# Node attention of a decoder: angle remainders moved from VectorE to GpSimd, mask matmuls of two query tiles in two row groups

## What is computed

```python
logits = (x @ wr).reshape(B, N, H, K_NODES).transpose(0, 2, 1, 3)
tk_vals, tk_idx = jax.lax.top_k(logits, TOP_K)
tk_w = jax.nn.softmax(tk_vals, axis=-1)
member = jax.nn.one_hot(tk_idx, K_NODES, dtype=jnp.float32).sum(axis=-2) > 0
pos = jnp.cumsum(m_i, axis=2) - m_i          # place of a token in its node
for n in range(K_NODES):
    p = pos[..., n]
    c = cos_c[p]
    s = sin_c[p]
    qr = q * c + _rotate_half(q) * s
    kr = k * c + _rotate_half(k) * s
    ...
```

## Time and profile before

| | us |
|---|---|
| median of 3 runs | 1866.5 (1866.48 to 1873.33) |
| the profiled execution, its own time | 1868.13 |
| its span, first to last instruction | 1866.4 |
| TensorE busy over the span | 1387.0 (74%) |
| VectorE busy | 1109.8 (59%) |
| ScalarE busy | 709.0 (38%) |
| GpSimd busy | 443.9 (24%) |
| mean granted TensorE clock | 0.863 of full |

### The profile page before, as it was taken

The page is one execution under the profiler, slowest core; times in us unless marked ns, Lnnn a source line. Parts: engine busy times, 40 slices in busy tenths (PEclk is TensorE's granted clock), DMA queues, the critical chain, the costliest instruction groups (busy, mean ns, idle before and its releaser), DMA issues. The chain is left out here.

```text
span 1866.4 us, 25316 instructions
## 1 busy us (share of the span) xinstructions
PE 1387.0 (74%) x9045; PEld 1055.8 (57%) x9045; DVE 1109.8 (59%) x2340; ACT 709.0 (38%) x1529; POOL 443.9 (24%) x464
## 2 busy tenths in 40 slices
PE   4898898888866897774765956758616878869785
PEld 3676666666745564561444955546513756646663
DVE  5899999999446577224566545352454827425534
ACT  4456666656222464221321221013203333634351
POOL 2565566565210100120101310000001015002300
PEclk8899899998878799786887977669868989989897
DMA  6111111010010100430002500000200002000100
GB/s 217 28 35 36 27 41 35 27 41 15 1 58 1 35 1 1 141 116 0 1 13 101 181 17 1 1 1 1 88 3 1 1 1 43 2 0 18 27 2 12
DMA packets 31612, 64.01 MB, mean 34 GB/s; under 512 B 6784, under 2 KB 18176, under 8 KB 30976
## 3 DMA queue, kind: packets, MB, share of 16 engines
q1 hardware_dynamic: 30464, 60.15, 10.4%
q0 software_dynamic: 1024, 2.23, 0.5%
HBM read 54.13 MB, written 4.18 MB: 31 GB/s over the span
## 5 line engine op out<-in xcount | busy, mean ns | idle before, releaser
L188 POOL TENSOR_TENSOR rstd<-spread,minus_half 128x4 f32<-128x4 f32 x36 | 36.9, 1024 | 913.2 <-DVE spread L170 913.2
L918 PE MATMUL l0h_scores<-l0h_k_rot,l0h_q_slots 128*128 128x128 f32 (+1 forms) x1024 | 208.2, 351 | 0.0
L918 PEld LDWEIGHTS l0h_scores<-l0h_k_rot,l0h_q_slots 128*128 128x128 f32 x1024 | 171.2, 210 | 13.3
L1135 POOL TENSOR_TENSOR l0h_k_part<-large_weights,l0h_sines 128x512 f32<-128x512 f32 x64 | 84.0, 1313 | 177.8 <-PE l0h_scores L918 129.8
L1009 ACT ACTIVATE l0h_scores<-l0h_scores,l0h_top 128x128 f32<-128x128 f32 (+1 forms) x256 | 100.6, 393 | 26.3 <-DVE l0h_top L1088 26.2
L1082 DVE TENSOR_TENSOR l0h_q_slots<-l0h_q_rot,l0h_chosen 128x1024 f32<-128x1024 f32 x64 | 78.4, 1225 | 6.7
L894 PE MATMUL l0h_projected<-XT,l0h_wq 128*128 128x256 f32 x256 | 70.1, 397 | 15.8 <-ACT large_weights L980 11.8
L1136 POOL TENSOR_TENSOR l0h_k_rot<-large_weights,l0h_cosines 128x512 f32<-128x512 f32 x64 | 81.0, 1266 | 0.0
L908 PE MATMUL l0h_scores<-l0h_key_masks,l0h_query_picks 4*128 4x128 bf16 (+1 forms) x256 | 45.2, 258 | 47.7 <-DVE l0h_probs L1105 47.7
L1447 ACT ACTIVATE l0n_probs<-l0n_scores,l0n_top 128x256 f32<-128x256 f32 x128 | 53.9, 483 | 38.9 <-DVE l0n_top L1478 38.7
L1088 DVE TENSOR_REDUCE l0h_top<-l0h_scores 128x2 f32<-128x256 f32 (+1 forms) x128 | 65.0, 546 | 5.4 <-PE l0h_scores L918 5.4
(11 more groups left out here) (761 smaller groups left out, 3703.6 us busy)
## 6 DMA issues: line engine op xcount, KB each, us to landing
l1e_experts<-in_l_experts SPq DMA_DIRECT2D x16, 768.0 KB, 4.3
l0e_experts<-in_l_experts SPq DMA_DIRECT2D x15, 578.0 KB, 3.9
l0h_chosen<-l0h_chosen_dram SPq DMA_DIRECT2D x64, 128.0 KB, 3.0
small_weights<-in_w_l_ffn SPq DMA_DIRECT2D x1, 4016.0 KB, 12.2
l0h_pos<-l0h_pos_dram SPq DMA_DIRECT2D x56, 64.0 KB, 2.1
large_weights<-in_w_l_xattn SPq DMA_DIRECT2D x1, 2632.0 KB, 9.1
l3f_late<-l3f_values SPq DMA_DIRECT2D x2, 1040.0 KB, 7.0
l0h_wq<-in_l_wq SPq DMA_DIRECT2D x16, 128.0 KB, 3.0
```

The lines of the kernel that those rows point to most:

```text
L918: mm = nc.tensor.matmul(at[:, slot], q_slots[:, s % 2, slot, part, i * P:(i + 1) * P], k_rot[:, s % 2, part, 0:KEYS[i][1]], start=False, s ...
L1135: nc.gpsimd.tensor_tensor(k_part[:], source, at_batch(sines, s), ALU.mult)
```

## The change

1. The remainders (`reduce_turns`) go from VectorE to GpSimd. VectorE keeps them for heads 0 and 1, before the loop. For heads 2 to 15 GpSimd computes them behind `rotate_k(s)` at b = 0 of the head before; until now VectorE did it at the end of the head two before.
2. On ScalarE `fold(h + 1)` stands at b = 0 (before: `fold(h + 2)` at b = 3), and `sines_of(h + 1)` at b = 1 (before: b = 0).
3. The masks lie twice in SBUF, at partitions 0 to 3 and 64 to 67. `load_masks` makes four transfers instead of two. The four mask matmuls of a step stand together ahead of both tiles, in the order tile 0, tile 1, tile 0, tile 1; tile 0 reads rows 0 to 3, tile 1 rows 64 to 67.

```diff
--- before.py
+++ after.py
@@ -787,8 +787,9 @@
         pos = sb("pos", [P, N], BF16)
         spread = sb("spread", [ROWS0, 2, NODES, FREQS], BF16)
         chosen = sb("chosen", [P, 2, CHOICES, N], BF16)
-        key_masks = sb("key_masks", [NODES, 2, N], BF16)
-        query_picks = sb("query_picks", [NODES, 2, CHOICES, N], BF16)
+        key_masks = sb("key_masks", [P // 2 + NODES, 2, N], BF16)
+        query_picks = sb("query_picks", [P // 2 + NODES, 2, CHOICES, N], BF16)
+        rows_of_tile = lambda i: slice(i * P // 2, i * P // 2 + NODES)
         cosines, sines = sb("cosines", [P, 2, N]), sb("sines", [P, 2, N])
         k_both = k.large_tail[:, 0:2 * N].rearrange("p (a n) -> p a n", a=2)
         k_rot, k_part = sb("k_rot", [P, 2, 2, S]), sb("k_part", [P, 2, S])
@@ -842,11 +843,12 @@
                 def load_masks(h):
                     if h >= 2:
                         sp.wait_ge(scores_ready, 2 * (h - 1) * B)
-                    sp.dma_start(key_masks[:, h % 2], absent_dram[h * NODES:(h + 1) * NODES])\
-                        .then_inc(masks_loaded[h % 2], 16)
-                    sp.dma_start(query_picks[:, h % 2],
-                                 chosen_dram[:, h * NODES:(h + 1) * NODES].rearrange("o r s -> r o s"))\
-                        .then_inc(masks_loaded[h % 2], 16)
+                    for i in range(TB):
+                        sp.dma_start(key_masks[rows_of_tile(i), h % 2], absent_dram[h * NODES:(h + 1) * NODES])\
+                            .then_inc(masks_loaded[h % 2], 16)
+                        sp.dma_start(query_picks[rows_of_tile(i), h % 2],
+                                     chosen_dram[:, h * NODES:(h + 1) * NODES].rearrange("o r s -> r o s"))\
+                            .then_inc(masks_loaded[h % 2], 16)
 
                 sp.dma_start(chosen_dram.rearrange("o r s -> r o s"), chosen_t[0:ROWS0]).then_inc(routes_stored, 16)
                 sp.dma_start(absent_dram, absent_t[0:ROWS0, :]).then_inc(routes_stored, 16)
@@ -900,14 +902,16 @@
                     h, b = step(s)
                     if s >= 2:
                         pe.wait_ge(combined, s - 1)
-                    pe.wait_ge(masks_loaded[h % 2], 32 * (h // 2 + 1))
+                    pe.wait_ge(masks_loaded[h % 2], 64 * (h // 2 + 1))
+                    for slot in range(CHOICES):
+                        for i in range(TB):
+                            query = slice((TB * b + i) * P, (TB * b + i + 1) * P)
+                            rows = rows_of_tile(i)
+                            nc.tensor.matmul(unit(scores, s, i)[:, slot], query_picks[rows, h % 2, slot, query],
+                                             key_masks[rows, h % 2, b * S:b * S + KEYS[i][1]], start=(slot == 0),
+                                             stop=False, skip_group_check=True)
                     for i in range(TB):
                         at = unit(scores, s, i)
-                        query = slice((TB * b + i) * P, (TB * b + i + 1) * P)
-                        for slot in range(CHOICES):
-                            nc.tensor.matmul(at[:, slot], query_picks[:, h % 2, slot, query],
-                                             key_masks[:, h % 2, b * S:b * S + KEYS[i][1]], start=(slot == 0), stop=False,
-                                             skip_group_check=True)
                         nc.tensor.matmul(at[:, :, i * P:(i + 1) * P], k.above[:], bc(k.masker[:].unsqueeze(1), [P, 2, P]),
                                          start=False, stop=False, skip_group_check=True)
                         if i == 0:
@@ -1044,11 +1048,11 @@
                     if k_chunk_at(s) is not None:
                         copy_k(4 * (s // (G0 * B) + 1) + k_chunk_at(s))
                     if b == 0 and 1 <= h < H0 - 1:
+                        fold(h + 1)
+                    if b == 1 and 1 <= h < H0 - 1:
                         sines_of(h + 1)
                     if b == 2 and h + 2 < H0:
                         turns(h + 2)
-                    if b == 3 and h + 2 < H0:
-                        fold(h + 2)
                 copy_turned(STEPS - 1)
                 copy_out(STEPS - 2)
                 copy_out(STEPS - 1)
@@ -1116,8 +1120,6 @@
                     if s + 2 < STEPS:
                         rotate_q(s + 2)
                     combine(s)
-                    if b == 3 and h + 2 < H0:
-                        reduce_turns(h + 2)
 
             @block.gpsimd
             def _(g):
@@ -1137,13 +1139,22 @@
                     nc.gpsimd.tensor_tensor(k_rot[:, s % 2, 0], k_rot[:, s % 2, 0], k_part[:, 1], ALU.subtract)
                     nc.gpsimd.tensor_tensor(k_rot[:, s % 2, 1], k_rot[:, s % 2, 1], k_part[:, 0], ALU.add).then_inc(k_rotated, 1)
 
+                def reduce_turns(h):
+                    g.wait_ge(turns_ready, h + 1)
+                    link(g, nc.gpsimd.tensor_scalar(sines[:, h % 2], cosines[:, h % 2], ROUND, ROUND, ALU.add, ALU.subtract))
+                    nc.gpsimd.tensor_tensor(sines[:, h % 2], sines[:, h % 2], cosines[:, h % 2], ALU.subtract)\
+                        .then_inc(turns_reduced, 1)
+
                 k.gchain(g, nc.gpsimd.memset(spread[:], 0.0))
                 for h in range(2):
                     nc.gpsimd.affine_select(out=spread[:, h], in_=spread[:, h], compare_op=ALU.not_equal, fill=1.0,
                                             base=-NODES * h, pattern=[[-1, NODES], [0, FREQS]], channel_multiplier=1)\
                         .then_inc(spread_set, 1)
                 for s in range(STEPS):
+                    h, b = step(s)
                     rotate_k(s)
+                    if b == 0 and 1 <= h < H0 - 1:
+                        reduce_turns(h + 1)
```

## The result

The changed kernel takes 1895.5 us, median of 4 runs (1891.82 to 1896.45), against 1869.9 for the kernel before, 4 runs too. The ratio is 1.013, 95% interval 1.0094 to 1.0165. The forecast was 1829, with a range of 1820 to 1847. The profiled execution took 1891.8 us, its span is 1890.1, 23.7 longer than before. The sixty steps of the attention that took 418.9 us now take 444.5, 25.6 more, so all of the loss lies there.

What follows compares the result with a forecast made beforehand. VectorE's list of work was taken as the bound. Terms -34.0 (remainder), -10 (stalls), +4.5 (K heads) and +2 (sines), the others 0, sum to -37.5 us, so 1829 us, range 1820 to 1847.

Steps and rivals of the forecast that it cites:

- The bound: VectorE's own list of work sets the stage's length nearly everywhere, 6.17 us per undisturbed step.
- The remainder leaves VectorE: On VectorE, 14 remainders of 2.43 us each disappear from its queue: -34.0 us.
- Stalls behind the falling clock: TensorE idles during VectorE's remainder, its clock falls, VectorE then waits; removing this gives -10 us, bounds 0 and -12.
- K heads: Three heads where TensorE has the longer chain, project_q awaiting ScalarE's key copy; +4.5 us over three, bounds +2 and +9.
- rival B: Only the remainder's time returns: clock still falls, or ScalarE ties late with VectorE; 1844 us, chance 0.30.
- Sines one step later: On ScalarE, cosines end just before VectorE's next product wants them, 0.03 us slack; +2 us, bounds 0 and +8.
- D: Time origin of the prediction's sums: the start of VectorE's first product in step b = 1.
- GpSimd, 0 us up to R = 6.5: GpSimd's remainder delays the keys of b = 1 only beyond R near 6.5; 0 us, bounds 0 and +41.
- R: Time of GpSimd's rounding and difference together per remainder: 3.9 us, bounds 3.2 and 9.4.
- 2.4 us of lead: How far TensorE's scores end before VectorE is free for them, counted as slack for late keys.
- Masks, 0 outside the K heads: Four mask matmuls together save TensorE 0.2 to 0.3 us a step, inside its slack of 0.67: 0 us.
- C: GpSimd becomes the bound: slower from R = 9.8, chance 0.04; another 0.04 for ending near no change.

Runs made afterwards that it cites:

- best_old_masks: late_sines_first with the masks as in the kernel before (one copy, tile by tile); 1837.1 us, 0.981 of before.
- masks_only: The kernel before with the masks' part of the change alone, remainders still on VectorE; 1863.6 us, 0.995 of before.
- no_remainder: The changed kernel without the remainders of heads 2 to 15 on any engine, sines still at b = 1; 1848.9 us, 0.987 of before.
- late_sines_first: The changed kernel with GpSimd's remainder behind the keys of b = 1 and the sines ahead of ScalarE's two copies; 1831.6 us, 0.979 of before.
- late_remainder: The changed kernel with GpSimd's remainder behind the keys of b = 1 instead of b = 0; 1852.0 us, 0.991 of before.
- sines_first: The changed kernel with the sines at b = 1 moved ahead of ScalarE's two copies; 1890.1 us, 1.009 of before.

## Why the prediction was wrong

**The bound.** Right: VectorE's list of 6.17 us a step is the floor, and all kernels return to it wherever nothing is late.

**The remainder leaves VectorE, -34.0.** Right: ahead of b = 0 the excess goes from 33.7 to 0.7.

**Stalls behind the falling clock, -10.** Right in size and, where nothing else is late, in cause: best_old_masks has no remainder on VectorE, the old masks and a clock of 1.00, and its 3.4 us ahead of b = 2 all lie in the K heads. The masks alone take 9.5 us away as well, with the clock still falling (b = 2 in masks_only), so the two gains do not add up. In the changed kernel new idle time of TensorE took the place of the old. Against rival B the prediction held that the step with `turns` leaves TensorE no idle time of 2.9 us. Behind VectorE's wait for the cosines that step (from 308.02) left it just that, and the eight scores behind it take 3.58 us and not 1.89:

```profile
313.42 0.39 PE L910 MATMUL l0h_scores<-l0h_key_masks,l0h_query_picks 4*128 4x128 bf16 x4 [2.92 <-DVE l0h_probs L1109]
...
314.87 3.58 PE L922 MATMUL l0h_scores<-l0h_k_rot,l0h_q_slots 128*128 128x256 f32 x8
```

**Sines one step later, +2, measured 32.5 ahead of b = 2.** First failed step: "ScalarE does its exponents and copies, loads the table at D + 2.75". That was read in the one step where the remainder on VectorE had put TensorE ahead, and the change removes that remainder. In a step without that lead it is D + 4.1 with the new masks, which alone costs 25 us (no_remainder; 22 of them without the K heads' own 3). The other 7 or 8 us come from TensorE being later still behind GpSimd: in the changed kernel the table of the step of 299.72 is loaded at 304.53, 4.8 us in.

**GpSimd, 0 us up to R = 6.5, measured 40.9 ahead of b = 1 at R = 6.0.** Second failed step, in three parts. R itself was mis-sized: 6.0 for 3.9, since the rounding took 3.63 us where I took 1.5; inside the bounds 3.2 to 9.4. The start was wrong: D + 10.1 was the end of keys that begin with the sines at D + 6.14; they began at 308.05, D + 8.3, and the remainder also waits for `turns`, which the sum left out. So TensorE gets the keys of b = 1 at 322.75, D + 23.0, where the prediction's own sum with R = 6.0 gives D + 20.1. These rows of the changed kernel show both, and what came of it:

```profile
304.53 1.28 ACT L1004 ACT_TABLE_LOAD   x1
...
308.05 1.27 POOL L1137 TENSOR_TENSOR l0h_k_part<-large_weights,l0h_sines 128x512 f32<-128x512 f32 x1 [6.13 <-ACT l0h_cosines L1005]
...
311.45 1.16 ACT L995 ACTIVATE l0h_cosines<-l0h_pos,large_weights 128x1024 f32<-128x1024 bf16 x1
...
312.70 3.63 POOL L1144 TENSOR_SCALAR l0h_sines<-l0h_cosines 128x1024 f32<-128x1024 f32 x1 [0.68 <-ACT l0h_cosines L995]
...
318.73 1.26 POOL L1137 TENSOR_TENSOR l0h_k_part<-large_weights,l0h_sines 128x512 f32<-128x512 f32 x1
...
322.75 1.16 PE L922 MATMUL l0h_scores<-l0h_k_rot,l0h_q_slots 128*128 128x128 f32 x8 [1.92 <-POOL l0h_k_rot L1140]
...
326.56 1.03 PE L896 MATMUL l0h_projected<-XT,l0h_wq 128*128 128x256 f32 x4
```

And the slack was measured to the wrong consumer. I gave TensorE 2.4 us of lead, from the end of its scores to `find_top`. But `project_q` stands last in TensorE's iteration, and VectorE takes it up right after: before, it ended at 331.4 and the next product but for the remainder stood at 326.70 + 6.17 = 332.9, a lead of 1.5. Here it ends at 327.59, and the product waits until 327.63.

**Masks, 0 outside the K heads.** Right where nobody is late (best_old_masks), and 0.3 us a step in the K heads as reckoned. Wrong for the two kernels compared here: 10.8 us of steps in masks_only (418.9 to 408.1), and 13 us beside the moved remainders (457.5 to 444.5), where TensorE is the late one. Slack is worth nothing only while nothing draws on it.

**K heads, +4.5.** About right: +5.1. In late_sines_first they stand nearly alone: 8.3 us beyond the floor, 7.8 of it theirs, 2.5 to 2.8 a head where I had reckoned 2.4 (before 0.9).

**The rivals.** C had the right mechanism for the larger part and the right sign, at the wrong threshold: it gave "no change" at R = 9.4, and with 0.08 for both parts too small a chance. B named the lost tie between ScalarE and VectorE, at half a microsecond a head where no_remainder shows 1.4. The forecast's time, 1829, is what late_sines_first measures, 1831.6: the gain was there, and two places in two queues gave it away. That the two times agree is no success of the forecast, which was for another kernel.

Shown by runs: the steps lose 29.4 us without any remainder and 74.3 with it, and the two moved calls together give back 66.0 (74.3 to 8.3). What each is worth depends on the other. Moving the remainder alone gives 42.6 (late_remainder) and moving the sines after that 23.4; moving the sines alone gives only 5.5 (sines_first). So 25 and 45 are shares in this order of taking the causes away, not two separate costs. Only argued: how much of the 45 is TensorE's half clock (at 350.71 in sines_first, for instance) and how much the bare wait; no kernel parted the two.

## What to carry to other kernels

When work moves to an engine with idle time, its busy share is not enough: write down what is queued behind the new place and when each consumer, down to the last thing in the consumer's own list, must have it; then try the next place in the queue as well. A slack read from one step is only good if the change leaves that step's conditions alone; read it in a step that already looks like the kernel after. Undo halves first: here one half was worth -0.5% and the other +1.95%, and moving two calls turned +1.3% into -2.1%.

## What was not expected of the hardware

GpSimd's rounding with two immediates took 3.63 us for 128 x 1024 float32, 1.5 times as long as its two-input difference (2.35), though it reads one operand. On VectorE the same pair takes 0.68 and 1.22 us at the shortest. The two engines no longer slowed each other: with VectorE's remainder gone none of `rotate_k`'s 64 last sums takes over 735 ns, where up to 1710 were seen before.
